# Four of the five shared-expert chunks ahead of the slot tiles instead of three

## The reference, cut to what matters

```
x = layernorm(h)                                   # 1216 x 256
shared_out = swiglu(x, shared_gate, shared_up, shared_down)      # every token, 256 -> 512 -> 256
logits = x @ gate_w.T;  top_id = argmax(logits)                  # 8 experts
score = sigmoid(max(logits));  xs = x * score[:, None]
for e in range(8):
    routed_out += swiglu(where(top_id == e, xs, 0), r_gate[e], r_up[e], r_down[e])
h = h + shared_out + routed_out
swiglu(x, wg, wu, wd) = silu(x @ wg.T) * (x @ wu.T) @ wd.T
```

## Time and profile before

| | |
|---|---|
| median of three timed runs | 574.7 us (573.93 to 576.48) |
| the profiled execution | 579.41 us |
| its span, first to last instruction | 577.6 us |
| busy: PE, DVE, ACT, POOL | 419.8, 324.2, 246.2, 143.9 us |
| mean granted TensorE clock | 0.832 of full |

### The profile page before, as it was taken

One profiled execution on the slowest core, in us unless ns is written; L12 is line 12 of the kernel. 1 busy time (PEld: TensorE's weight loads), 2 busy tenths in 40 slices (PEclk: granted clock), 3 DMA queues, 4 the chain that ended last, 5 costly groups with the idle time before them and its releaser, 6 DMA issues.

```text
span 577.6 us, 8904 instructions
## 1 busy us (share of the span) xinstructions
PE 419.8 (73%) x3189; PEld 306.6 (53%) x3189; DVE 324.2 (56%) x876; ACT 246.2 (43%) x512; POOL 143.9 (25%) x169
## 2 busy tenths in 40 slices
PE   3677884477779979999889993362497114699997
PEld 3545652256568965666555782221243013489996
DVE  3858875489653410232411116868898995645642
ACT  4235444256634411222212211396099476286661
POOL 3544433089721150000000053800000000213410
PEclk9969887569997997999999998685555555599999
DMA  8921111293003332111101071000000000000002
GB/s 278 406 99 17 20 17 14 82 425 167 2 1 146 111 109 83 36 56 37 49 25 43 23 291 37 0 1 3 1 1 0 1 2 2 1 1 0 1 19 68
DMA packets 19789, 38.59 MB, mean 67 GB/s; under 512 B 2136, under 2 KB 16164, under 8 KB 18340
## 3 DMA queue, kind: packets, MB, share of 16 engines
q1 hardware_dynamic: 18788, 35.41, 17.7%
q0 software_dynamic: 960, 2.62, 1.3%
HBM read 29.77 MB, written 7.01 MB: 64 GB/s over the span
## 4 chain that ended last, share of the span: by engine, by line
PE 46%; DVE 28%; issue 11%; ACT 8%; POOL 5%; DMA 2%; SPq 1%; DVEq 0%; ACTq 0%
PE psum L1253 11%; PE psum L1285 5%; PE psum L2334 4%; PE psum L2367 3%; PE psum L1260 3%; POOL ring L782 2%; PE psum L1299 2%; PE psum L610 2%; PE psum L2373 2%; ACT experts L1662 1%; POOL experts L787 1%; PE psum L921 1%; PE psum L1277 1%; DMA experts<-in_tern 1%; PE psum L2351 1%
## 5 line engine op out<-in xcount | busy, mean ns | idle before, releaser
L1253 PE MATMUL psum<-experts,ring 128*128 x136 | 67.1, 619 | 1.6 <-issue 1.2
L1084 DVE TENSOR_TENSOR ring<-ring,psum 128x512 f32<-128x512 f32 x17 | 11.7, 688 | 67.9 <-PE psum L1253 67.9
L1184 POOL DMA_INDIRECT front<-expert_results,slot_of x10 | 9.5, 953 | 126.4 <-DMA expert_results<-ring 123.7
L1260 PE MATMUL psum<-front,shared 128*128 128x256 f32 (+1 forms) x160 | 36.8, 383 | 0.0
L1253 PEld LDWEIGHTS psum<-experts,ring 128*128 128x128 f32 x136 | 24.4, 199 | 21.0 <-issue 20.9
L1260 PEld LDWEIGHTS psum<-front,shared 128*128 128x128 f32 x160 | 30.3, 197 | 3.5
L1285 PE MATMUL psum<-experts,ring 128*128 x136 | 32.1, 379 | 0.0
L1285 PEld LDWEIGHTS psum<-experts,ring 128*128 128x128 f32 x136 | 25.8, 190 | 10.3 <-issue 7.7
L1382 ACT COPY ring<-psum 128x512 f32<-128x512 f32 x17 | 10.0, 586 | 42.3 <-PE psum L1277 42.3
L2334 PE MATMUL psum<-experts 128*128 128x256 f32 (+1 forms) x120 | 27.4, 371 | 0.0
L590 PE MATMUL psum<-experts,ring 128*128 128x256 f32 x108 | 26.1, 393 | 0.8 <-DVE experts L485 0.7
(11 more groups left out here) (361 smaller groups left out, 1085.7 us busy)
## 6 DMA issues: line engine op xcount, KB each, us to landing
experts<-in_experts SPq DMA_DIRECT2D x8, 1536.0 KB, 12.5
experts<-in_x SPq DMA_DIRECT2D x9, 384.0 KB, 8.3
expert_rows<-zeros SPq DMA_DIRECT2D x1, 2176.0 KB, 14.8
ring<-expert_rows SPq DMA_DIRECT2D x17, 128.0 KB, 2.2
shared<-in_shared SPq DMA_DIRECT2D x1, 1536.0 KB, 18.0
experts<-in_ffn_q SPq DMA_DIRECT2D x1, 1536.0 KB
experts<-in_ffn_s SPq DMA_DIRECT2D x1, 1536.0 KB
experts<-in_pos_embed SPq DMA_DIRECT2D x1, 1152.0 KB, 9.6
```

Of the source, the lines that this page charges most:

```text
L1084: nc.vector.tensor_tensor(o, o, up_bank(g), ALU.mult).then_inc(hidden_done.sem, 1)
L1253: mm = nc.tensor.matmul(bank, sl_xT[t % 2][:, k, :], slot_w(t, block, k, F), start=(k == 0), stop=(k == KD - 1))
L1260: mm = nc.tensor.matmul(o[:, b, 0:w], shared_w(block, k, (2 * half + b) * P, P), moe_x(c)[:, k, 0:w], start=(k == 0), stop=(k == KD - 1))
```

## The change

```
-        MOE_EARLY = 3
+        MOE_EARLY = 4
         SHARED_EARLY = 2 * MOE_EARLY
```

## The result

| | before | after |
|---|---|---|
| median, first comparison | 575.9 us (573.93 to 577.01, 15 runs) | 573.08 us (569.42 to 575.0, 15 runs) |
| ratio | | 0.9952, interval 0.9933 to 0.9972 |
| profiled execution, span | 579.41, 577.6 us | 570.71, 568.9 us |

The gain was 2.8 us where 5.2 were forecast. The two profiles are 8.7 us apart. Nearly 3 us of that lies ahead of the change: the first scatter is issued at 199.80 in the profile of before and at 196.82 in that of after. So I count both profiles from that issue, which neither kernel moves against the work ahead of it. Counted so, the profile of after is 5.7 us shorter.

A forecast was written before the change was run, and what follows sets the result against it. Bound: PE's 3.5 us wait for slot rows plus 2.9 us slow clock, and at the back the fourth chunk. Rows stage 5.2 us earlier: 579.41 − 5.2 = 574.2 profiled, 574.7 − 5.2 = 569.5 timed; range includes 566.5, up to 573.3.

The forecast's parts named there:

- Front: Ahead of slot tile 0: the 3.49 us wait goes, full clock holds, the slot tiles start 3.78 us later.
- Last slot tile: Around the last tile's transposition: 0.86 us less work, so the last slot down product ends 2.92 us later, at 335.87.
- Gathers bind: Start of the rows stage: set by the first gathers at 347.4, later than the 346.07 PE would allow.
- the fifth addition: Rows stage on DVE: the fifth pair is added 8.24 us behind the first, at 355.7.
- 344.5: Time taken for the first gather pair's landing before the change; shifted by 2.92 us it gives 347.4.
- thin cover: Rows stage: POOL makes its first root by 352.4, DVE wants it at 353.0; 0.6 us to spare.
- The start that it was measured from: Rows stage before the change: starts at 352.65, 7.60 us behind 345.05; the forecast start was 5.2 us earlier.
- The carry-over: Whole kernel: the profile's 5.2 us gain taken unchanged off the timed median of 574.7, giving 569.5 us.
- Rival two: Slot tile 0: the slow clock was no gain; 2.9 us less, gain 2.3, 572.4 us; chance 20%.
- Rival three: Rows stage: gather issues and DVE additions contend for the shared port; gain about 3.4, 571.3 us; chance 14%.
- a sign of being wrong: Rows stage: gather issues above 1.2 us or L1553 additions further than 1.9 us apart would count against the forecast.
- Rival four: PE's restarts, as before layer 1: the clock comes back later; 5.2 us slower, 579.9 us; chance 6%.

The follow-up runs named there:

- e1: Kernel before with seven extra 128x256 products filling TensorE's wait for slot tile 0's rows; 0.9957 against before, 2.76 us less.
- e13: Kernel before, unchanged, run once more on another chip; ratio 0.9983 against a median of 580.67 us.
- e4: All five shared chunks ahead of the slot tiles (MOE_EARLY = 5); 1.010 against before, slower.
- e3: Changed kernel with the two feed-forward loads issued only after all gathers have landed; 0.9903 against before, 3.5 us less than the changed kernel.
- e2: Changed kernel, same file, run again on another chip than the before-at-580 ones; 573.41 us, 0.9968 against before.
- e10: Changed kernel, same file, on a chip where before took 580.28 us; 573.77 us, 0.9883 against before.
- e15: Changed kernel, same file, on a chip where before took 580.67 us; 574.16 us, 0.9880 against before.
- e18: Changed kernel, same file, on a chip where before took 580.3 us; 573.08 us, 0.9887 against before.

## Why the prediction went wrong, step by step

- **Front: right.** From the first scatter's issue, the first L1253 was forecast at 24.97 us (224.77 − 199.80) and came at 24.92; the L1269 behind slot tile 0 at 31.87, and it came at 31.90. The wait is gone, the clock stayed up, and e1 shows the price of the slow clock alone: 3.0 us in the profile (last slot down product at 130.32 against 133.32) and 2.76 us in the timed runs. The price varies: the eight L1253 records took 6.2 to 6.6 us in four of the five profiles of before and 4.9 in e13.
- **Last slot tile: right.** The down product was forecast 2.92 us later; it ends at 136.28 against 133.32, 2.96 later.
- **Gathers bind: right.** The first L1553 was forecast at 147.6 behind the scatter and came at 147.56, released by a gather; the fifth addition at 155.9, and it came at 155.84. That it was met to 0.04 us is luck: 344.5 was a middle between 343.9 and 345.0, and the other four profiles of the changed kernel have 147.7 to 147.9. e4 (10.67 us idle for gathers) and e3 (the gathers sooner without the loads) show the same mechanism. POOL's first root was ready in time, as forecast with thin cover; in e3 that cover was gone and cost 2.04 us.
- **The start that it was measured from: wrong.** The step that failed is "From that point to the rows stage it was 345.05 to 352.65, 7.60 us, with the late product on DVE in it". I took the late product (347.46, "remote", rows 4) as a part of the kernel before. It is a late signal, which the profile of before has and the timed chip need not have. e1, with the same order at the back, takes 5.5 us for that stretch and has the stage start 17.4 us behind the down product, where before had 19.5. The forecast start of 347.4, set by the gathers, does not move with it. What moves is the start that it is compared with, from 352.65 to about 350.5. So in the first comparison 2.1 us of the 5.2 were most likely not there to win, and 3.1 remain; measured were 2.8 there and 2.55 in e2. The first profile of the changed kernel points the same way: its L1089 at the front stands at 12.79 behind the scatter, as in e1 to e4, that of before at 14.29, as on the other four chips. No profile of the kernel before itself was taken where it takes 576, so the 2.1 rests on e1 and on the medians.
- **The carry-over: wrong.** "The timed runs lack something of it, perhaps part of the slow clock" named the doubt at the wrong place. The slow clock is in the timed runs, as e1 shows. The profile most likely stood 4.7 us above the median of 574.7 because before takes 4 us more on some chips, and the profile shows the late signals of those. There the gain was larger than forecast: 6.5 to 7.2 us by the medians beside e10, e15 and e18, against 5.2.
- **Rival two** named a gain of 2.3 us, for a reason right in form (the timed runs lack a stall of the profile) and with the wrong stall. That 2.3 came near the measured 2.8 is chance. **Rival three**, the shared port: in after the three gather issues beside DVE's additions took 0.94 to 1.02 us, and the additions stand 1.9 us apart as before. In other profiles of the same kernel the issue that starts within the first addition is stretched, to 1.38 us in e2 and 1.34 in e15, which is above the 1.2 that I had named as a sign of being wrong. The addition keeps its 0.69, and DVE never waits for POOL's first root. So the contention is there and costs this kernel nothing: the rival's loss didn't come. Timeline of DVE, then of POOL, in e2:

```profile
347.00 0.69 DVE L1553 TENSOR_TENSOR h<-h,front 128x512 f32<-128x512 f32 x1 [3.67 <-DMA front<-expert_results,slot_of]
```

```profile
347.13 1.38 POOL L1184 DMA_INDIRECT front<-expert_results,slot_of  x1 [0.30 <-issue]
```

- **Rival four**: the half clock before the projection was longer in after, but the projection's start to the next step (L1678 to L1714) took 17.3 us against 17.4; no loss.

## What to carry over

In this kernel it paid to fill the tensor engine's wait with just as much work as it is long. Half a chunk took the wait and the slow clock away and left the gathers covered, where a whole chunk pushed the slot tiles back by 3.8 us and laid the gathers bare. Before a stall in a profile becomes a term of the sum, ask what releases it: one that ends on nothing the program does is not sure to be in the timed runs, and a sum that holds it needs both values in its range. And before a profile is set against timed runs, ask whether both come from the same chip: here one kernel took 576 us on one chip and 580 on four others.

## What the hardware showed beyond that

On four of the five chips of e1 to e18, signals of PE reached DVE late, at two places, both while a burst of indirect DMAs runs. At the front, all fourteen profiles from these chips have DVE's L1089 at 14.3 to 14.5 us behind the first scatter, where the other chip has 12.8. At the back DVE starts 0.3 to 3.0 us later than it does on the other chip, in all kernels with three or three and a half early chunks. On the fifth chip no profile had one. The front is in the profile of before too: DVE's product at 214.09 was such a one, hidden under PE's wait. What delays the signals was not found. Each chip was used in one group of runs, so chip and time of the runs can't be told apart.

The five profiles of the changed kernel have none at the back, on either kind of chip. There PE's last shared product ends 4.2 us behind the issue of the first gather and is signalled on time. The late ones ended 9.0 us behind it (three chunks) and 10.3 us behind it (half a chunk). So the change moved PE's last signals out of the stretch in which they come late. That fits its time, 573.1 to 574.2 us on every chip; no run was made to test this alone.

The load of weights has a price far from itself: GpSimd's unpacking beside DVE's operations on six columns stretched L1614 from 0.21 to 0.65 us and more, and e3, in which the unpacking came late, was 3.5 us faster than the changed kernel. The Trainium skill ("SBUF — State Buffer", "Who interferes with whom") says that a vector instruction in a 2-port mode contends with GpSimd and that one with two SBUF inputs contends with a GpSimd instruction that reads SBUF. The stretched operations agree with it: L1618, which has two SBUF inputs, took 0.96 us in e2, beside GpSimd's L2243, and 0.25 in e3. Which of the two cases L1614 is, no run shows. The issue of a gather that started within a two-input addition took up to 1.39 us (e3), one that started 0.1 us ahead of it 0.95.
